# Both ends of a DLRM tower on one core: another treatment of a few contraction units in rounds -1, 0, 1, 29 and 30

## The chip, the core and the metric

The kernel runs on one NeuronCore of a Trainium2 chip. The metric is the device time of one execution in microseconds (us), the median of several runs. The engines are TensorE (PE; its weight loads are PEld), VectorE (DVE), ScalarE (ACT), GpSimd (POOL) and SyncE (SP), which issues most of the DMAs.

## What is computed

From 39 embedding tables rows of 16 numbers are gathered for a batch of 1024, giving `x` of 1024 x 39 x 16. Three layers of a compressed interaction network follow, and a small dense tower:

```python
def _cin(x, Ws, bs):
    h = x
    for i, (W, b) in enumerate(zip(Ws, bs)):
        Wr = W.reshape(F0, Fk, L)                              # L = 128
        z = jnp.einsum('bfd,bgd->bfgd', x, h)                  # products of every field with every row of h
        cur = jax.nn.relu(jnp.einsum('bfgd,fgl->bld', z, Wr) + b[None, :, None])
        if i != n - 1:
            h = cur[:, :L // 2]; direct = cur[:, L // 2:]
        else:
            direct = cur
        outs.append(direct)
    return jnp.concatenate(outs, axis=1).sum(-1)
...
h = jnp.concatenate([z, dense_ctx], axis=1)
h = jnp.maximum(h @ W_top1 + b_top1, 0.0)
h = jnp.maximum(h @ W_top2 + b_top2, 0.0)
y = h @ W_top3
```

## The kernel before, in words

The 1024 x 16 columns (batch, d) are cut into 32 steps of 512 columns. A step passes through layer 0, layer 1 and layer 2 in successive rounds: round `r` does layer 1 of step r+1 (units 0 to 9, `A_END`), layer 2 of step r (units 10 to 19, `C_END`) and layer 0 of step r+3 (units 20 to 23). Rounds run from -3 to 31; those at the ends lack some parts (`present`, line 57). Each unit is a pair of tiles of 128 products by 512 columns. VectorE makes the products `z` of a unit (line 628 for layers 1 and 2, line 679 for layer 0) and TensorE contracts them with the weights into one PSUM bank, over the ten units of a layer. ScalarE then applies bias and relu and writes `h1` or `h2`, the factor of the next layer's products, and the `direct` or `last` half, which VectorE sums over d (line 719).

How a unit is contracted depends on its kind (`KINDS`, `kind`, line 65):

- **F**, full: one fp32 matmul a tile, `wf` with `z` (line 1004). The trace records two instructions for each.
- **G, D, P**, split: ScalarE rounds `z` to `zh` (fp32r, line 826), a subtraction makes `zl = z - zh`, and TensorE adds three products a tile in fp32r: `wl` with `zh` (L1021), `wh` with `zh` (L1022), `wh` with `zl` (L1029). In G the subtraction is GpSimd's (L367), in D VectorE's (L715). In P the product goes to a PSUM bank half a unit at a time, and VectorE makes product (L694) and subtraction (L706) of each half, ScalarE rounding between (L811).

The order of the work is written out: each engine walks the rounds and units in the same order and waits on semaphores that count units. `z` has 7 buffers, `zh` and `zl` 4 each. VectorE does a D unit's subtraction `lag(r)` units after its product (1 before round 0, then 4, 2 in the last round). The second half of a P unit follows `half_lag` units later (line 109: 1 in round 30, otherwise 2). Before round 1 all split units are D, since P's bank is in use and GpSimd is busy: its queue holds 77 gathers of embedding rows ahead of its first subtraction, which is unit 11 of round 0. The last 38 of these wait for products of rounds -2 and -1 (`BESIDE`, line 148) and the two behind them. A few F units get split weights later (`wh_late`, `wl_late`): made by ScalarE and GpSimd in round 1 (unit 4, called `TENTH`) and in round 25 (units 3, 8, 14, 19).

In round 30 ScalarE writes the four later strips of `h2` (line 860) between its roundings; the `last` half of layer 2 (`take2`) stands at unit 1 of each round and waits for TensorE's last unit of the round before. After round 30 come the dense layers of the tower, then round 31 (layer 2 of the last step) and the last 128 rows.

## Time and profile before

| what | value |
|---|---|
| median of 3 runs | 1277.16 us (1276.98 to 1277.82) |
| profiled execution, own time | 1275.78 us |
| its span, first to last instruction | 1274.0 us |
| busy, share of the span | PE 95%, DVE 87%, POOL 84%, ACT 65% |
| mean granted TensorE clock | 0.997 |

All durations below come from the one profiled execution. Busy time counts instructions with work; a wait is idle time, and the profile names what ended it. TensorE's matmuls are pipelined, so a row of one matmul lasts longer than the distance to the next; the distance is what it costs in a row of them.

### The profile page before, as it was taken

What the parts mean: (1) busy time and instruction counts of PE and PEld (TensorE: products, weight loads), DVE (VectorE), ACT (ScalarE), POOL (GpSimd) and SP (SyncE); (2) the same over time, 40 slices, a digit from 0 to 9 for tenths busy, and PEclk for the clock granted to TensorE, in tenths of its full rate; (3) what the DMA queues carried; (4) which work ended last, traced back from release to release, by engine and by line L of the source; (5) the groups of instructions that cost most, each with busy time, mean ns of one, the idle gap of its engine ahead of it and who ended that gap; (6) DMA issues with size and microseconds to landing.
All of it is one profiled execution on the core that took longest, in us unless ns stands there. A gap on an engine that the chain in (4) does not pass through costs nothing.

```text
span 1274.0 us, 14489 instructions
## 1 busy us (share of the span) xinstructions
PE 1208.4 (95%) x4206; PEld 770.9 (61%) x4206; DVE 1113.7 (87%) x1274; ACT 829.4 (65%) x1129; POOL 1068.3 (84%) x643
## 2 busy tenths in 40 slices
PE   0588999999999999999999999999999999999899
PEld 0244566666666666666666666666666666766555
DVE  2189999899989999899999999899999999999763
ACT  1147666667676767666666767667766778777553
POOL 7467988898999999898999999898999878887533
PEclk9999999999999999999999999999999999999999
DMA  9194466654545556655545666554545666544100
GB/s 187 22 229 103 106 144 148 148 127 115 130 104 123 141 148 148 147 110 123 132 107 125 145 147 148 140 121 112 134 102 136 143 146 145 145 110 118 44 1 1
DMA packets 102511, 156.18 MB, mean 123 GB/s; under 512 B 20811, under 2 KB 32988, under 8 KB 102322
## 3 DMA queue, kind: packets, MB, share of 16 engines
q1 hardware_dynamic: 92256, 152.56, 50.0%
q0 software_dynamic: 10176, 2.70, 2.3%
q8 instruction: 33, 0.54, 0.2%
q14 instruction: 46, 0.38, 0.1%
HBM read 151.31 MB, written 6.19 MB: 124 GB/s over the span
## 4 chain that ended last, share of the span: by engine, by line
PE 82%; DVE 6%; POOL 4%; issue 4%; ACT 3%; DMA 0%; another core or an unknown queue 0%; DVEq 0%; ACTq 0%; POOLq 0%
PE curM L1004 35%; PE curM L1029 14%; PE curM L1021 14%; PE curM L1022 14%; POOL emb L356 3%; DVE z L628 3%; PE xk L993 2%; ACT h L860 1%; DVE zl L715 1%; ACT zh L826 1%; DVE zl L706 1%; POOL zl L367 1%; DVE z L679 0%; PE h L1127 0%; PE h L1135 0%
## 5 line engine op out<-in xcount | busy, mean ns | idle before, releaser
L367 POOL TENSOR_TENSOR zl<-z,zh 128x1024 fp32r<-128x1024 f32 (+1 forms) x314 | 749.7, 2398 | 106.6 <-ACT zh L826 94.1
L826 ACT ACTIVATE zh<-z 128x1024 fp32r<-128x1024 f32 (+1 forms) x333 | 351.5, 1057 | 312.4 <-DVE z L628 184.9
L628 DVE TENSOR_TENSOR z<-xr,h 128x1024 f32<-128x1024 f32 x456 | 548.7, 1212 | 3.8 <-issue 3.1
L1004 PE MATMUL curM<-z,wf 128*128 128x512 f32 (+3 forms) x1164 | 513.4, 600 | 0.9 <-ACT h L860 0.8
L356 POOL DMA_INDIRECT emb<-in_tbl_dram,idx x312 | 311.4, 998 | 88.1 <-issue 58.4
L1021 PE MATMUL curM<-zh,wl 128*128 128x512 f32 (+1 forms) x816 | 367.8, 451 | 4.0 <-issue 1.8
L1004 PEld LDWEIGHTS curM<-z,wf 128*128 128x128 f32 (+3 forms) x1164 | 204.2, 188 | 223.4 <-issue 206.5
L1022 PE MATMUL curM<-zh,wh 128*128 128x512 f32 (+1 forms) x816 | 320.5, 393 | 0.0
L1029 PE MATMUL curM<-zl,wh 128*128 128x512 f32 (+1 forms) x816 | 255.3, 394 | 10.3 <-POOL zl L367 6.0
L860 ACT ACTIVATE h<-curM,bias 64x512 f32<-64x512 f32 x372 | 240.4, 646 | 22.6 <-DVE z L628 11.2
L706 DVE TENSOR_TENSOR zl<-curY,zh 128x512 fp32r<-128x512 f32 x240 | 165.0, 688 | 63.5 <-ACT zh L811 58.5
L1021 PEld LDWEIGHTS curM<-zh,wl 128*128 128x128 f32 (+1 forms) x816 | 154.4, 189 | 59.8 <-issue 26.6
L1022 PEld LDWEIGHTS curM<-zh,wh 128*128 128x128 f32 (+1 forms) x816 | 153.8, 189 | 54.1 <-issue 26.1
L1029 PEld LDWEIGHTS curM<-zl,wh 128*128 128x128 f32 (+1 forms) x816 | 152.4, 188 | 51.2 <-POOL zl L367 8.7
L694 DVE TENSOR_TENSOR curY<-xr,h 128x512 f32<-128x512 f32 x240 | 166.1, 692 | 4.1
L811 ACT ACTIVATE zh<-curY 128x512 fp32r<-128x512 f32 x240 | 141.5, 590 | 15.8 <-PE curM L1029 6.5
L679 DVE TENSOR_TENSOR z<-xk,xs 117x1024 f32<-117x1024 f32 x116 | 120.7, 1081 | 1.2 <-PE curM L1004 1.2
L628 DVE TENSOR_TENSOR z<-xq,h 128x1024 f32<-128x1024 f32 x64 | 77.5, 1212 | 0.0
L860 ACT ACTIVATE direct<-curM,bias 64x512 f32<-64x512 f32 x62 | 42.4, 684 | 1.6
L993 PEld LDWEIGHTS xk<-ident,emb 128*117 128x117 f32 x120 | 28.5, 285 | 13.2 <-issue 8.5
L1021 PE MATMUL curM<-zh,wl_late 128*128 128x512 f32 x72 | 35.1, 487 | 0.0
L715 DVE TENSOR_TENSOR zl<-z,zh 128x1024 fp32r<-128x1024 f32 (+1 forms) x19 | 28.7, 1509 | 5.7 <-ACT zh L826 3.9
(140 smaller groups left out, 428.8 us busy)
## 6 DMA issues: line engine op xcount, KB each, us to landing
xr<-xT SPq DMA_DIRECT2D x384, 192.0 KB
xs<-xT SPq DMA_DIRECT2D x279, 156.0 KB
xq<-xT SPq DMA_DIRECT2D x64, 256.0 KB
emb<-in_tbl_dram,idx POOLq DMA_INDIRECT x312
xs<-xT SPq DMA_DIRECT2D x62, 78.0 KB
xT<-xc SPq DMA_DIRECT2D x31, 78.0 KB
xr<-in_L_rec_W_dram SPq DMA_DIRECT2D x16, 144.0 KB
xT<-xc SPq DMA_DIRECT2D x31, 40.0 KB
```

The lines of the kernel that those rows point to most:

```text
L356: nc.gpsimd.indirect_dma_start(out=emb[slot][:, f * D:(f + 1) * D], out_offset=None, in_=tables[f], in_offset=bass.IndirectOffsetOnAxis(ap ...
L367: nc.gpsimd.tensor_tensor(zl[0:n, SNUM[r, u] % NL, :], z[0:n, z_slot(r, u), :], zh[0:n, SNUM[r, u] % NH, :], ALU.subtract).then_inc(lo_poo ...
L628: return nc.vector.tensor_tensor(z[:, slot, :].rearrange("p (a n) -> p a n", a=2), x, h, ALU.mult)
L694: nc.vector.tensor_tensor(curY[:, :], xr[s % 2][:, q * N:(q + 1) * N], h[:, a * N:(a + 1) * N], ALU.mult).then_inc(done, 1)
L706: nc.vector.tensor_tensor(zl[:, SNUM[r, u] % NL, cols], curY[:, :], zh[:, SNUM[r, u] % NH, cols], ALU.subtract).then_inc(lo_dve if a == 1 ...
L811: nc.scalar.activation(zh[:, SNUM[r, u] % NH, a * N:(a + 1) * N], curY[:, :], ACT.Copy).then_inc(hi_ready if a == 0 else hi_second, 1)
L826: nc.scalar.activation(zh[0:n, SNUM[r, u] % NH, :], z[0:n, z_slot(r, u), :], ACT.Copy).then_inc(hi_ready, 1)
L860: nc.scalar.activation(dst, src, ACT.Relu, bias=bias).then_inc(done, 1)
L1004: mm = nc.tensor.matmul(cur[:, :], wf[rows, full_at(u), a, :], z[rows, z_slot(r, u), a * N:(a + 1) * N], start=start and i == 0, stop=stop ...
L1021: nc.tensor.matmul(cur[:, :], w_low[rows, w, a, :], zh[rows, h, cols], start=start and a == 0, stop=False)
L1022: nc.tensor.matmul(cur[:, :], w_high[rows, w, a, :], zh[rows, h, cols], start=False, stop=False)
L1029: mm = nc.tensor.matmul(cur[:, :], w_high[rows, w, a, :], zl[rows, l, a * N:(a + 1) * N], start=False, stop=stop and a == n - 1)
```

## The change

In the kinds, per round (before, then changed; kinds of units 0 to 9, 10 to 19, 20 to 23; all other rounds stay):

```
 -1 DDDFFDDDFF .......... FDFF      FEDFFDEDFF .......... FDFF
  0 DDDFFDDDFF FGDGFFGDGF FGFF      FEDFFDEDFF FGEGFFGEGF FGFF
  1 GPGFFGPGFF FGPGFFGPGF FGFF      FPGFFGPGFF FGPGFFGPGF FGFF
 29 GPGGFGPGFF FGPGGFGPGF ....      GPGFFGGGFF FGPGGFGGGF ....
 30 GPGGFGPGFF FGPGGFGPGF ....      FPGFFGGGFF FGPGGFGGGF ....
```

- A new kind **E** for units 1, 6, 12 and 17 before round 1: TensorE takes the high weights with all of `z` in fp32 and the low weights with `zh`; no `zl` is made. A buffer of `z` is then free only when TensorE is done with it.
- Unit 0 (`HEAD`) is F in rounds -1, 0, 1 and 30, and uses late split weights, made in round 1, in rounds 2 to 29.
- In rounds 29 and 30 unit 3 is F, and units 6 and 17 are G in place of P (`HANDED`).
- D units of round 0 have a lag of 2 in place of 4. The second half of a P unit always follows 2 units later.

```diff
-KINDS = "GPGFFGPGFF" + "FGPGFFGPGF" + "FGFF"
+KINDS = "FPGFFGPGFF" + "FGPGFFGPGF" + "FGFF"
...
-TENTH = 4
-LATE = (TENTH,) + LATE_C + LATE_A
-SHORT, LONGER = (STEPS - 3, STEPS - 2), (8, 19)
+HALF = 2
+TENTH, HEAD = 4, 0
+EARLY = (TENTH, HEAD)
+LATE = EARLY + LATE_C + LATE_A
+SHORT, LONGER, HANDED = (STEPS - 3, STEPS - 2), (3, 8, 19), (6, 17)
...
 def kind(r, u):
-    if r in SHORT and u in LONGER:
-        return "F"
-    if u == TENTH and 3 <= r < LATE_FROM and r % 4 != 2:
+    if r in SHORT and u in LONGER + HANDED:
+        return "F" if u in LONGER else "G"
+    if u == TENTH and 2 < r < LATE_FROM and r % 4 != 2:
+        return "G"
+    if u == HEAD and 2 <= r < STEPS - 2:
         return "G"
...
     if k == "P":
-        return "P" if r in IN_PSUM else "D"
+        return "P" if r in IN_PSUM else "E" if r < 1 else "D"
...
 def lag(r):
-    return 1 if r < 0 else 2 if r == LAST else 4
+    return 1 if r < 0 else 2 if r in (0, LAST) else 4
...
-def half_lag(r):
-    return 1 if r == STEPS - 2 else 2
...
 def behind(r, u, halves):
-    for n in (1, 2):
-        at = NUM[r, u] - n * halves
-        if at >= 0 and ORDER[at] in HALVES and half_lag(ORDER[at][0]) == n:
-            return ORDER[at]
-    return None
+    at = NUM[r, u] - HALF * halves
+    return ORDER[at] if at >= 0 and ORDER[at] in HALVES else None
...
(GpSimd; ScalarE the same with weight_hi_late)
-                    if (r, u) == (1, 2):
-                        weight_lo_late(0)
-                    if r == LATE_FROM and 2 <= u < 1 + len(LATE):
-                        weight_lo_late(u - 1)
+                    if r == 1 and 2 <= u < 2 + len(EARLY):
+                        weight_lo_late(u - 2)
+                    if r == LATE_FROM and 2 <= u < 2 + len(LATE) - len(EARLY):
+                        weight_lo_late(u - 2 + len(EARLY))
...
(VectorE, z_free)
-                if before is not None and kind(*before) == "F":
+                if before is not None and kind(*before) in "EF":
                     dve.wait_ge(z_used, NUM[before] + 1)
...
(TensorE, contract)
+                    if kind(r, u) == "E":
+                        pe.wait_ge(z_ready, NUM[r, u] + 1)
+                        for a in range(n):
+                            nc.tensor.matmul(cur[:, :], w_high[:, w, a, :].bitcast(F32), z[:, z_slot(r, u), a * N:(a + 1) * N],
+                                             start=start and a == 0, stop=False)
                     pe.wait_ge(hi_ready, SNUM[r, u] + 1)
+                    for a in range(n if kind(r, u) == "E" else 0):
+                        mm = nc.tensor.matmul(cur[:, :], w_low[:, w, a, :], zh[:, h, a * N:(a + 1) * N], start=False,
+                                              stop=stop and a == n - 1)
+                    if kind(r, u) == "E":
+                        mm.then_inc(z_used, 1)
+                        return
```

What VectorE issues for units 0 to 9 of round -1, before (`z` from `xr`, `xq` and `h` is a product, `zl` a subtraction):

```order
L628 TENSOR_TENSOR z<-xr,h 128x1024 x2
L715 TENSOR_TENSOR zl<-z,zh 128x1024
L628 TENSOR_TENSOR z<-xr,h 128x1024
L715 TENSOR_TENSOR zl<-z,zh 128x1024
L628 TENSOR_TENSOR z<-xr,h 128x1024
L715 TENSOR_TENSOR zl<-z,zh 128x1024
L628 TENSOR_TENSOR z<-xr,h 128x1024 x3
L715 TENSOR_TENSOR zl<-z,zh 128x1024
L628 TENSOR_TENSOR z<-xr,h 128x1024
L715 TENSOR_TENSOR zl<-z,zh 128x1024
L628 TENSOR_TENSOR z<-xr,h 128x1024
L715 TENSOR_TENSOR zl<-z,zh 128x1024
```

and the same place in the changed kernel, where the lines are numbered one lower:

```order
L627 TENSOR_TENSOR z<-xr,h 128x1024 x4
L714 TENSOR_TENSOR zl<-z,zh 128x1024
L627 TENSOR_TENSOR z<-xr,h 128x1024 x3
L714 TENSOR_TENSOR zl<-z,zh 128x1024
L627 TENSOR_TENSOR z<-xr,h 128x1024 x2
L714 TENSOR_TENSOR zl<-z,zh 128x1024
```

Six subtractions have become three, those of units 2, 5 and 7; the product of unit 9 (from `xq`) follows directly in both.

TensorE at the start of round 0, changed (the transposes of L992, then units 0, 1 and 2; before, all three units were the five rows that unit 2 still has):

```order
L992 MATMUL xk<-ident,emb 117x128 x4
L1003 MATMUL curM<-z,wf 128x512 x2
L1017 MATMUL curM<-z,wh 128x512 x2
L1021 MATMUL curM<-zh,wl 128x512 x2
L1031 MATMUL curM<-zh,wl 128x512
L1032 MATMUL curM<-zh,wh 128x512
L1031 MATMUL curM<-zh,wl 128x512
L1032 MATMUL curM<-zh,wh 128x512
L1039 MATMUL curM<-zl,wh 128x512 x2
```

Unit 0 needs `z` alone, and unit 1 (E) needs `zh` only for its last two matmuls.

ScalarE in round 30, units 0 to 3, before (`h` are the strips of `h2`, `last` waits for the end of round 29; `zh` from `curY` are halves of P unit 1):

```order
L860 ACTIVATE h<-curM,bias 64x512 x2
L811 ACTIVATE zh<-curY 128x512
L860 ACTIVATE last<-xk,bias 128x512
L860 ACTIVATE h<-curM,bias 32x512 x2
L811 ACTIVATE zh<-curY 128x512
L826 ACTIVATE zh<-z 128x1024
L860 ACTIVATE h<-curM,bias 32x512 x2
```

and changed:

```order
L859 ACTIVATE h<-curM,bias 64x512 x2
L810 ACTIVATE zh<-curY 128x512
L859 ACTIVATE last<-xk,bias 128x512
L859 ACTIVATE h<-curM,bias 32x512 x2
L825 ACTIVATE zh<-z 128x1024
L859 ACTIVATE h<-curM,bias 32x512 x2
L810 ACTIVATE zh<-curY 128x512
```

Unit 1's second half has moved behind `zh` of unit 2 and the last two strips of `h2`.

## Rows read from the trace of the kernel before

**Rows 1.** The page: busy us, share of the span and instructions of each engine.

```profile
PE 1208.4 (95%) x4206; PEld 770.9 (61%) x4206; DVE 1113.7 (87%) x1274; ACT 829.4 (65%) x1129; POOL 1068.3 (84%) x643
```

**Rows 2.** Stretches: length, busy of each engine (instructions), granted clock, DMA share, GB/s.

```profile
78.00:152.00 74.00, 63.15 (x194) 35.96 (x194) 70.94 (x64) 44.47 (x56) 62.17 (x44) 0.98 0.63 139
152.00:188.10 36.10, 36.10 (x125) 22.81 (x124) 34.51 (x40) 24.24 (x34) 31.86 (x21) 1.00 0.58 131
1186.40:1223.30 36.90, 31.84 (x110) 19.09 (x108) 26.77 (x32) 20.93 (x28) 21.33 (x9) 1.00 0.00 1
110.00:114.00 4.00, 3.71 (x10) 2.94 (x11) 4.00 (x5) 1.06 (x1) 3.39 (x3) 0.57 0.06 4
```

**Rows 3.** The chain of waits: start us, us, what; rounds -1 and 0.

```profile
95.91 3.40 DVE z L679 x3
...
137.16 3.43 PE curM L1004 x8
```

**Rows 4.** Timeline of VectorE: start us, us, instruction, count, idle before; rounds -1, 0.

```profile
77.47 2.35 DVE L628 TENSOR_TENSOR z<-xr,h 128x1024 f32<-128x1024 f32 x2 [3.06 <-issue]
...
111.28 1.22 DVE L715 TENSOR_TENSOR zl<-z,zh 128x1024 fp32r<-128x1024 f32 x1
...
123.75 5.75 DVE L628 TENSOR_TENSOR z<-xr,h 128x1024 f32<-128x1024 f32 x5
129.41 3.71 DVE L715 TENSOR_TENSOR zl<-z,zh 128x1024 fp32r<-128x1024 f32 x1
```

**Rows 5.** Timeline of TensorE, round 0 and the start of round 1.

```profile
108.11 0.47 PE L1021 MATMUL curM<-zh,wl 128*128 128x512 f32 x1 [1.78 <-issue]
...
132.08 0.74 PE L1029 MATMUL curM<-zl,wh 128*128 128x512 f32 x2 [1.86 <-POOL zl L367]
...
136.43 0.72 PE L1029 MATMUL curM<-zl,wh 128*128 128x512 f32 x2 [1.31 <-POOL zl L367]
...
141.81 0.39 PE L1021 MATMUL curM<-zh,wl 128*128 128x512 f32 x1
...
143.18 0.39 PE L1021 MATMUL curM<-zh,wl 128*128 128x512 f32 x1
...
151.94 0.87 PE L993 MATMUL xk<-ident,emb 128*117 128x128 f32 x4
```

**Rows 6.** GpSimd: its 38 gathers of 71 to 129.65 us grouped, then its timeline.

```profile
L356 POOL DMA_INDIRECT emb<-in_tbl_dram,idx x38 | 47.2, 1243 | 30.0 <-DVE z L679 19.4 <-issue 7.3 <-DVE z L628 3.4
...
100.90 0.94 POOL L356 DMA_INDIRECT emb<-in_tbl_dram,idx  x1 [0.30 <-issue]
...
111.36 1.96 POOL L356 DMA_INDIRECT emb<-in_tbl_dram,idx  x1 [0.30 <-DVE z L628]
...
129.66 2.37 POOL L367 TENSOR_TENSOR zl<-z,zh 128x1024 fp32r<-128x1024 f32 x1
132.18 1.77 POOL L356 DMA_INDIRECT emb<-in_tbl_dram,idx  x1 [0.16 <-issue]
```

**Rows 7.** Timeline of ScalarE, rounds -1 and 0: the activations into `h1` and `h2`.

```profile
95.94 4.00 ACT L860 ACTIVATE h<-curM,bias 64x512 f32<-64x512 f32 x6 [2.76 <-DVE z L628]
...
102.88 4.00 ACT L860 ACTIVATE h<-curM,bias 64x512 f32<-64x512 f32 x6 [1.25 <-DVE z L679]
```

**Rows 8.** Timeline of ScalarE, round 30.

```profile
1187.04 0.69 ACT L860 ACTIVATE last<-xk,bias 128x512 f32<-128x512 f32 x1 [2.15 <-PE xk L1004]
...
1189.01 0.57 ACT L811 ACTIVATE zh<-curY 128x512 fp32r<-128x512 f32 x1
```

**Rows 9.** Timeline of VectorE, round 30.

```profile
1191.97 0.69 DVE L719 TENSOR_REDUCE zq<-direct 128x128 f32<-128x512 f32 x1 [0.47 <-ACT h L860]
...
1205.93 0.69 DVE L706 TENSOR_TENSOR zl<-curY,zh 128x512 fp32r<-128x512 f32 x1 [1.07 <-ACT zh L811]
...
1217.80 1.21 DVE L628 TENSOR_TENSOR z<-xr,h 128x1024 f32<-128x1024 f32 x1
```

**Rows 10.** Timeline of TensorE, round 30: the start of unit 2.

```profile
1190.99 0.40 PE L1021 MATMUL curM<-zh,wl 128*128 128x512 f32 x1
```

More of the change, by code:

```diff
@@ L477, in round_ @@
                         for u in range(A_END + 3 * k + 1, A_END + 3 * k + 4):
-                            if kind(r, u) == "P" and u + half_lag(r) > A_END + 3 * k + 3:
+                            if kind(r, u) == "P" and u + HALF > A_END + 3 * k + 3:
                                 sp.wait_ge(z_second, HALVES[r, u] + 1)
@@ L910, in round_ @@
                             take0(r, i)
-                    if (r, u) == (1, 2):
-                        weight_hi_late(0)
-                    if r == LATE_FROM and 2 <= u < 1 + len(LATE):
-                        weight_hi_late(u - 1)
+                    if r == 1 and 2 <= u < 2 + len(EARLY):
+                        weight_hi_late(u - 2)
+                    if r == LATE_FROM and 2 <= u < 2 + len(LATE) - len(EARLY):
+                        weight_hi_late(u - 2 + len(EARLY))
                     if u == SPREAD_AT and r >= 1 and fresh(r) and r <= STEPS - 4:
@@ L1011, in contract @@
                         w, w_low, w_high = LATE.index(u), wl_late, wh_late
-                        if r <= LATE_FROM + 1 and (u != TENTH or r < 6):
+                        if r <= LATE_FROM + 1 and (u not in EARLY or r < 6):
                             pe.wait_ge(w_hi, HI_OPS + w + 1)
                             pe.wait_ge(w_lo, LO_OPS + w + 1)
-                    pe.wait_ge(hi_ready, SNUM[r, u] + 1)
+                    if kind(r, u) == "E":
[3 more added lines that the diff above has]
+                                             start=start and a == 0, stop=False)
+                    pe.wait_ge(hi_ready, SNUM[r, u] + 1)
+                    for a in range(n if kind(r, u) == "E" else 0):
[4 more added lines that the diff above has]
+                        return
                     for a in range(n):
```

## The prediction

> **What bounds the kernel now.** The page comes first [rows 1]: TensorE 95% busy, VectorE 87%, GpSimd 84%, so shares alone leave three candidates. The table by stretches separates them [rows 2]: in the 36.1 us of round 1, which stand for all the rounds up to 29, TensorE is busy for the whole stretch, so there only its own work counts. It idles in two places: rounds -1 and 0 (78 to 152 us: 63.2 of 74 us) and round 30 (1186.4 to 1223.3: 31.8 of 36.9 us). The change edits just these ends. All times below are on the clock of the trace of before.
>
> In round -1 the wait chain runs through VectorE, from 77.47 up to 95.91 [rows 3, 4]: products and subtractions (`zl`) follow one another without a gap. A product occupies it for 1.13 us (five from 123.75, next start 129.41), a subtraction for as long (1.22 with its overlap, like a product's 1.21) [rows 4]. In round 0 TensorE waits for GpSimd: for its subtraction of unit 11, begun at 129.66 behind the gathers, until 132.08, and for unit 13 until 136.43 [rows 5, 6]. From then on the chain is TensorE's own work [rows 3].
>
> **Prices on TensorE.** Two full units (F) take 3.43 us: 1.72 each [rows 3]. A three-pass unit (D, G, P) repeats after 141.81 at 143.18: 1.37, or 0.229 for each of its six matmuls of 512 columns [rows 5]. F in place of a three-pass unit costs 0.35. The new kind E has the fp32 matmuls of F and two short passes: 1.72 + 0.46 = 2.18, +0.81. No row shows an E; it lies between 1.72 (the short matmuls free) and 3.09 (they cost a whole three-pass unit), and since both parts have rows of their own shape I take 2.18. Weight loads lie beside the matmuls (PEld 61% busy) [rows 1]. Six E and six extra F are 4.9 + 2.1 = 7.0 us of new TensorE work.
>
> **Round -1.** Units 0, 1, 6 lose their subtractions, 3 x 1.13 = 3.4 us of VectorE's unbroken row. Unit 9's product releases the `h1` activations (95.94, 4.00 us); behind them stand `zh` of unit 21, its subtraction, the product of unit 23, and that releases the `h2` activations at 102.88, done at 106.88 [rows 7]. All are in one chain, so they move 3.4 earlier: 103.5. TensorE fits beneath: from 78.7, when unit 0's product (77.47, 1.2 us) is there, round -1 is 5 F + 2 E + 3 D = 17.1 us and 5.7 for units 20 to 23, ending near 101.5. Before, unit 0 of round 0 needed `zh` and started at 108.11 [rows 5]; as F it starts at 103.5.
>
> **Round 0 up to unit 11.** TensorE: 17.1 us for units 0 to 9, 1.72 for unit 10, 0.92 for unit 11's first passes: 123.2. GpSimd: 38 gathers stand ahead of its subtraction for unit 11 [rows 6]. One takes 0.94 and the pause 0.30, 1.25 together; all 38 took 47.2 us, 11.5 more than 38 x 0.94. The twelve long ones (up to 1.96) each start inside a VectorE subtraction and end 0.8 after it: 111.36 to 113.32 against the subtraction 111.28 to 112.50 [rows 4, 6]. Thirteen subtractions fall there now, seven remain (units 2, 5, 7 twice, and 21, which cost nothing before). Laying gathers of 1.25 us beside the new VectorE order gives extensions of 0.7, 0.8, 0.9, 0.4, 0.9, 0.9: 4.6 us. Bounds: 0 (all missed) and 6 x 1.02 = 6.1. So GpSimd is 11.5 - 4.6 = 6.9 us earlier (5.4 to 11.5), and unit 11's low part comes at 125.2. That is after TensorE's 123.2: GpSimd still decides, by 2.0 us.
>
> The Trainium skill (SBUF — State Buffer, section "SBUF: two separate sides") says a VectorE instruction with two SBUF inputs blocks only a GpSimd instruction that reads SBUF, and names two-port modes as what starves a DMA issued by GpSimd. By it these fp32 subtractions would not lengthen a gather, and the start would keep its 132.08; the rows above say otherwise, and I go by them.
>
> **Round 0 from unit 11.** Before, 132.08 to the end at 151.94 is 19.9 us, with 1.3 of waiting at unit 13. That wait came from the gather at 132.18 (1.77) inside unit 12's subtraction, itself held to 3.71 us by GpSimd [rows 4, 6]. Unit 12 is now E: no subtraction, and the wait goes. Two E add 1.6. 19.9 - 1.3 + 1.6 = 20.2: the round ends 6.9 - 0.3 = **6.6 us earlier**. VectorE sheds eight subtractions in the two rounds, but past unit 11 that wins nothing: it runs up against the seven `z` buffers and waits for TensorE. The lag of 2 instead of 4 for D units of round 0 costs nothing: `zh` of unit 2 is ready 2 units later. The loads for round 1 hang on ScalarE's `xc` copy of round 0, which moves along with unit 7, so they stay ahead of a round 1 that begins near 145.
>
> **Rounds 1 to 29.** TensorE-bound: unit 0 of round 1 costs +0.35, unit 3 of round 29 +0.35. One more pair of late weights (0.7 us on GpSimd, 0.4 on ScalarE) replaces a subtraction of 2.4 and one `zh`. Units 6 and 17 of round 29 go to GpSimd, 11 x 2.37 = 26.1 us in 29.4: hidden, with little spare.
>
> **Round 30.** TensorE ends round 29 at 1187.0, where it releases ScalarE's `last` [rows 8]; now at 1187.4. With the lag of one, unit 1's second half followed two activations (1189.01); with the lag of two it comes after `last`, two activations, `zh` of unit 2 and two more: 0.7 + 1.3 + 1.05 + 1.3 + 0.6, ready at 1192.4. VectorE's `zq` still waits for the last `h2` activation (1191.97) [rows 9], then comes unit 4's product, then unit 1's last half: 1194.3. So TensorE does unit 0 and half of unit 1, **idles 2.9 us and again 1.4**, and starts unit 2 at 1194.8 where it was 1190.99 [rows 10]: 3.8 later. Behind it, before, lay waits of 5.5 us (1190.99 to 1223.3 against 6 x 1.72 + 12 x 1.37 = 26.8), because VectorE stood 1.07 us at units 6, 12 and 17 and had half products besides [rows 9]. Now units 6 and 17 are whole and unit 12 has its lag: VectorE ends the round at about 1213 (1192.5 with 15 products, 5 halves and one sum behind) instead of 1219, ahead of TensorE. 7 x 1.72 + 11 x 1.37 = 27.1, plus 0.5 where GpSimd does units 5, 6, 7 in a row (3 x 2.37 from 1196.5, when units 4 and 5 have their products and `zh` is made, to 1203.6): 1222.4. Against 1223.3 a **gain of 0.9**, round 29's 0.35 included. Bounds: all 5.5 us stay, 1227.4 (4.1 lost); unit 1 does not wait, 1187.4 + 30.2 = 1217.6 (5.7 won). Round 31 and the top layers follow at TensorE's pace, unchanged.
>
> **Sum.** 6.6 - 0.35 + 0.9 = 7.1 us. The profiled execution took 1275.78 (span 1274.0): now 1268.7. The median of 1277.16, 1.4 above it, becomes 1270.1. A measurement of this kernel tells 0.2% from no change: 2.6 us, so faster means below 1274.6.
>
> **Rivals.**
> - First, the gathers miss the subtractions, and TensorE alone sets the start. Round 0 ends at 103.5 + 17.1 + 16.7 + 5.7 = 143.0, 8.9 earlier: 1267.7. For it: extension depends on phase. Chance 0.13.
> - Second, the wait at unit 1 of round 30 is much shorter than I lay out, up to 5.7 won there: 6.6 - 0.35 + 5.7 = 12.0, 1265.2. Against it: ScalarE works in program order. 0.07.
> - Third, the gathers are as long as before. Unit 11 gets its part at 132.1, and the sum is -0.3 - 0.35 + 0.9: 1276.9. This is also what the Trainium skill's rule above gives. Twelve rows in twelve speak against it. 0.07.
> - Fourth, the waits of round 30 stay behind the new one: 6.6 - 0.35 - 4.1 = 2.15 won, 1275.0. For it: GpSimd has ten subtractions there, as many as before. 0.08.
> - Fifth, slower: the clock. After waits in round 0 the granted clock was 0.57 in 110 to 114 us, mostly the 1.2 GHz level, where it is 1.00 in round 30 [rows 2]. The new waits in round 30 look alike. Priced as there it is (1 - 0.57) x 4 = 1.7 us, within my range. It turns the sign where over 9.7 us of full-speed work run at half; for half of the 27 us behind the wait, +13.5: 1283.6. 0.04. The Trainium skill (TensorE: Matmul & The Clock Gate, Part 1) has idleness bring back the half rate and activity lift it.
>
> The forecast keeps 0.61. Faster: 0.61 + 0.13 + 0.07, and what of the fourth lies beyond the limit, 0.83. Same: the third and most of the fourth, 0.13. Slower: 0.04. The range goes past the first rival on one side and to the fourth on the other, the start's lower bound (1.5 less) and the clock's 1.7 within it: 1266 to 1275.
>
> **What would show it.** TensorE's first F of round 0 near 103.5; the first GpSimd subtraction near 123 instead of 129.66; round 0's end near 145.5; long gathers six, not twelve. In round 30, an idle of some 3 us at unit 1 and hardly any after. Wrong if GpSimd's first subtraction does not move, if VectorE waits for loads before 103 us, or if round 30 keeps its later waits.

## The result, and the profile after

| | before | changed |
| --- | --- | --- |
| median of 4 runs, us | 1277.07 (1276.89 to 1277.82) | 1290.16 (1285.03 to 1296.93) |
| ratio | 1 | 1.011, 95% interval 1.008 to 1.0139 |
| profiled execution, us (span) | 1275.78 (1274.0) | 1286.04 (1284.0) |
| mean granted clock | 0.997 | 0.989 |

The change makes the kernel 13.1 us slower, and its runs scatter over 12 us where those of before lie within 1. Forecast were 1270.1 us and faster. Two executions of the changed kernel lie near 1285.5 (one is the profiled one) and two near 1295.6 (clock 0.984 and 0.985).

TensorE's transposes (L992, L993 before) open each round, so they date it (start in us). Before: round 0 at 105.46, round 1 at 151.94, round 28 at 1122.06, end at 1274.0. Changed: 102.62, 160.33, 1130.86, 1284.0. So round 0 opened 2.8 us earlier, **round 0 took 57.7 us in place of 46.5**, rounds 1 to 27 together 0.4 longer, and the rest 1.2 longer.

The page of the changed kernel, busy us and share of each engine, as [rows 1]:

```profile
PE 1216.3 (95%) x4194; PEld 772.3 (60%) x4194; DVE 1096.0 (85%) x1254; ACT 823.6 (64%) x1120; POOL 1060.5 (83%) x644
```

Stretches of the changed kernel: length, busy of each engine, granted clock, DMA share, GB/s, as [rows 2]:

```profile
78.00:103.00 25.00, 24.63 (x71) 12.80 (x69) 23.16 (x21) 14.37 (x19) 19.56 (x18) 1.00 1.00 227
103.00:161.00 58.00, 44.09 (x125) 24.14 (x125) 37.43 (x37) 27.91 (x37) 32.13 (x26) 0.85 0.39 84
116.70:133.80 17.10, 6.75 (x13) 3.31 (x12) 9.17 (x9) 5.32 (x8) 4.03 (x5) 0.50 0.16 34
161.00:197.00 36.00, 36.00 (x121) 21.99 (x121) 34.21 (x40) 24.42 (x34) 32.65 (x21) 1.00 0.54 131
1202.20:1209.00 6.80, 5.88 (x11) 3.81 (x12) 6.52 (x7) 3.17 (x3) 3.57 (x2) 0.50 0.00 0
```

In round -1 TensorE is busy for 24.6 of 25 us, as was wanted. In round 0 nobody is busy: TensorE 44 of 58 us, VectorE 37, GpSimd 32. In such a stretch the engines wait for one another, so the chain of waits has to be followed. The granted clock lies at 0.50, the 1.2 GHz level, for 17.1 us there and for 6.8 us in round 30.

Timeline of VectorE in round 0, as [rows 4]; idle time before in brackets:

```profile
105.05 1.20 DVE L627 TENSOR_TENSOR z<-xr,h 128x1024 f32<-128x1024 f32 x1
106.18 1.22 DVE L714 TENSOR_TENSOR zl<-z,zh 128x1024 fp32r<-128x1024 f32 x1
113.67 1.22 DVE L627 TENSOR_TENSOR z<-xr,h 128x1024 f32<-128x1024 f32 x1 [6.27 <-PE curM L1003]
116.50 1.22 DVE L627 TENSOR_TENSOR z<-xr,h 128x1024 f32<-128x1024 f32 x1 [1.61 <-issue]
125.64 1.22 DVE L627 TENSOR_TENSOR z<-xr,h 128x1024 f32<-128x1024 f32 x1 [7.93 <-remote]
126.78 1.22 DVE L714 TENSOR_TENSOR zl<-z,zh 128x1024 fp32r<-128x1024 f32 x1
```

Timeline of TensorE, the same stretch, as [rows 5]:

```profile
104.10 1.98 PE L1003 MATMUL curM<-z,wf 128*128 128x512 f32 x4 [0.61 <-issue]
...
109.49 3.59 PE L1003 MATMUL curM<-z,wf 128*128 128x512 f32 x8
116.03 0.50 PE L1031 MATMUL curM<-zh,wl 128*128 128x512 f32 x1 [2.95 <-issue]
...
128.06 1.22 PE L1039 MATMUL curM<-zl,wh 128*128 128x512 f32 x2 [10.28 <-DVE zl L714]
```

Timeline of GpSimd, as [rows 6]: the last of the 38 gathers, and GpSimd's first subtraction:

```profile
121.00 0.94 POOL L355 DMA_INDIRECT emb<-in_tbl_dram,idx  x1 [0.30 <-issue]
134.91 2.37 POOL L366 TENSOR_TENSOR zl<-z,zh 128x1024 fp32r<-128x1024 f32 x1 [12.96 <-ACT zh L825]
```

The three rows of products with a bracket are units 5, 6 and 7 of round 0. They wait for nothing but their buffer of `z` (unit 6 also for a load of `xr`, landed at 102.39): seven buffers back lie units 22 and 23 of round -1 and unit 0 of round 0, all F, whose buffer is free when TensorE has counted them in the semaphore `z_used`. (A count, below, is such an update of a semaphore.) Unit 0 ran from 104.10 on. Yet unit 7's product, which needs its count, starts at 125.64. TensorE stands still meanwhile, 10.28 us, for the subtraction of unit 5, which is in VectorE's queue behind the product of unit 7. So what is missing is the count. The trace records when TensorE's semaphores are raised; beside them, the end of the last matmul of each unit (not printed by the views, read from the same trace, us):

```
                               last matmul ends   count arrives   late
before   round 0, unit 0            111.51            114.87       3.4
         round 0, unit 1            113.91            114.94       1.0
         round 0, unit 3            117.27            117.28       0.0
changed  transposes of round 0      103.49            123.50      20.0
         round 0, unit 0            106.08            125.62      19.5
         round 0, unit 1            108.26            125.70      17.4
         round 0, unit 4            113.08            125.89      12.8
         round 0, unit 5            129.28            129.29       0.0
```

TensorE's counts arrive up to **20 us late**, in order, and then five in 0.27 us. Some 100 of the 768 counts of `z_used` have no record. A record belongs to the latest unit that the records behind it leave for it, or to an earlier one, so each lateness of `z_used` here is the least that it can be. In steady state, and from 129 us on, they come 0.01 to 0.02 us after the matmul. Before the change there was a lateness too, of 3.4 us, and it cost little. The Trainium skill (Perfetto Trace Analysis, section "Tensor Engine Instruction (MATMUL, LD_WEIGHTS)") has the count pushed when the last bytes in PSUM are acknowledged, and the end of a matmul in a profile only estimated. The steady rounds agree; no rule of it gives the 20 us.

### The profile page after: what moved, and what is told of

Read it like the earlier page. It is cut to its first block, busy times and chain, and to the rows that moved or that the text cites. A ratio compares the mean times of both kernels' runs of the same rounds, so it can differ in the third digit from the quotient of the medians.

```text
span 1284.0 us, 14414 instructions
## 1 busy us (share of the span) xinstructions
PE 1216.3 (95%) x4194; PEld 772.3 (60%) x4194; DVE 1096.0 (85%) x1254; ACT 823.6 (64%) x1120; POOL 1060.5 (83%) x644
## 4 chain that ended last, share of the span: by engine, by line
PE 89%; DVE 3%; issue 3%; POOL 2%; ACT 2%; another core or an unknown queue 1%; DMA 0%; DVEq 0%; ACTq 0%
PE curM L1003 38%; PE curM L1039 14%; PE curM L1031 14%; PE curM L1032 14%; POOL emb L355 2%; PE xk L992 2%; DVE z L627 2%; ACT h L859 1%; PE curM L1017 1%; PE h L1089 1%; PE curY L1003 1%; ACT zh L825 1%; DVE zl L705 1%; PE h L1137 0%
## 5 line engine op out<-in xcount | busy, mean ns | idle before, releaser
L1003 PE MATMUL curM<-z,wf 128*128 128x512 f32 (+3 forms) x1188 | 525.7, 601 | 1.9 <-issue 1.0
L1031 PE MATMUL curM<-zh,wl 128*128 128x512 f32 (+1 forms) x740 | 335.3, 453 | 5.7 <-issue 2.9
L1032 PE MATMUL curM<-zh,wh 128*128 128x512 f32 (+1 forms) x740 | 290.8, 393 | 0.1
L1039 PE MATMUL curM<-zl,wh 128*128 128x512 f32 (+1 forms) x740 | 230.8, 393 | 11.6 <-DVE zl L714 10.3
L705 DVE TENSOR_TENSOR zl<-curY,zh 128x512 fp32r<-128x512 f32 x232 | 159.5, 687 | 57.7 <-ACT zh L810 52.6
L1031 PEld LDWEIGHTS curM<-zh,wl 128*128 128x128 f32 (+1 forms) x740 | 139.7, 189 | 59.1 <-issue 28.4
L1032 PEld LDWEIGHTS curM<-zh,wh 128*128 128x128 f32 (+1 forms) x740 | 139.7, 189 | 52.0 <-issue 25.8
L1039 PEld LDWEIGHTS curM<-zl,wh 128*128 128x128 f32 (+1 forms) x740 | 139.5, 189 | 44.7 <-DVE zl L714 11.2
L1031 PE MATMUL curM<-zh,wl_late 128*128 128x512 f32 x124 | 58.3, 470 | 0.0
L1032 PE MATMUL curM<-zh,wh_late 128*128 128x512 f32 x124 | 48.6, 392 | 0.0
L1039 PE MATMUL curM<-zl,wh_late 128*128 128x512 f32 x124 | 38.5, 392 | 0.0
```

What stands on the lines that cost most here:

```text
L705: nc.vector.tensor_tensor(zl[:, SNUM[r, u] % NL, cols], curY[:, :], zh[:, SNUM[r, u] % NH, cols], ALU.subtract).then_inc(lo_dve if a == 1 ...
L1003: mm = nc.tensor.matmul(cur[:, :], wf[rows, full_at(u), a, :], z[rows, z_slot(r, u), a * N:(a + 1) * N], start=start and i == 0, stop=stop ...
L1031: nc.tensor.matmul(cur[:, :], w_low[rows, w, a, :], zh[rows, h, cols], start=start and a == 0, stop=False)
L1032: nc.tensor.matmul(cur[:, :], w_high[rows, w, a, :], zh[rows, h, cols], start=False, stop=False)
L1039: mm = nc.tensor.matmul(cur[:, :], w_high[rows, w, a, :], zl[rows, l, a * N:(a + 1) * N], start=False, stop=stop and a == n - 1)
```

## The experiments

Theory A at this point: E and F units free their buffer by TensorE's late count, D units by VectorE's own, so E turns a harmless lateness into a standstill. The rival, B, is the end (round 30, at half clock for 6.8 us). In the diffs `-` is the change as made, or the kernel that the text names as the one started from. The table of all runs is at the end of this section.

**Halves of the change.** Only the start:

```diff
-SHORT, LONGER, HANDED = (STEPS - 3, STEPS - 2), (3, 8, 19), (6, 17)
+SHORT, LONGER, HANDED = (STEPS - 3, STEPS - 2), (8, 19), ()
-    if u == HEAD and 2 <= r < STEPS - 2:
+    if u == HEAD and 2 <= r:
```

with `half_lag` of before.

> The change's start (E in rounds -1 and 0, unit 0 as F there, lag 2 in round 0) with the end of before (SHORT, LONGER, HANDED, half_lag, unit 0 as G in rounds 29 and 30). Theory A: the loss is VectorE's standstill in round 0, where it waits for TensorE's count of used buffers (6.3, 1.6 and 7.9 us in the trace of the change), and the half clock that follows: this kernel then lies at 1277 plus 8.8 (what the change's trace is behind at round 28), near 1286 and as scattered as the change (1285 to 1297). Rival B: the end carries the loss, since round 30 of the change has 6.8 us at the lower clock level: this kernel then lies near 1270.

Measured 1287.12 us (1284.72 to 1297.53). The start alone carries the loss; rival B falls. The profiled execution is the slowest of the five, and in it the standstill is not in round 0, as theory A had it, but already in round -1: VectorE waits for counts from 92 us on, 8.92 and 7.17 us the longest, and round 0 opens only at 121.34. Where the standstill falls differs from one execution to another; the scatter of the changed kernel may be the same thing, but none of its slower executions was traced.

**No E**, lag 4 in round 0:

```diff
-        return "P" if r in IN_PSUM else "E" if r < 1 else "D"
+        return "P" if r in IN_PSUM else "D"
-    return 1 if r < 0 else 2 if r in (0, LAST) else 4
+    return 1 if r < 0 else 2 if r == LAST else 4
```

> The change without E: units 1, 6, 12, 17 of rounds -1 and 0 are D again and round 0 has lag 4; unit 0 stays F in rounds -1 to 1 and the end stays as changed. Theory A (E's buffers are freed by TensorE's count instead of VectorE's own, and that is what makes VectorE stand): back to within 2 us of before, 1274 to 1278. Rival B (the end or unit 0 as F loses): 1279 or more. Rival C (any F more in round 0 makes VectorE wait by TensorE's count): a standstill of VectorE in round 0 stays, of over 3 us.

Measured 1284.57 (1283.64 to 1285.07). Theory A falls as stated: without a single E, VectorE stands at the product of unit 10, as rival C foresaw, for an F unit's count:

```profile
129.08 1.22 DVE L627 TENSOR_TENSOR z<-xq,h 128x1024 f32<-128x1024 f32 x1 [8.96 <-remote]
```

**E in round -1 alone** (`"E" if r < 0`, lag 4 in round 0).

> E in round -1 alone; round 0 has D and lag 4 as before. Theory A: round -1 keeps its gain (the first product of round 0 2.8 us earlier than in before) and VectorE's buffers of round 0 come free by its own subtractions: 1272 to 1275, faster than before. Rival B (E itself is dear wherever it stands, or delays TensorE's count already in round -1): 1277 or more, with a wait of VectorE of over 3 us in round 0.

Measured 1289.45 (1286.98 to 1296.51). Now it is ScalarE that waits for a late count, between rounds, for unit 9 of round -1:

```profile
113.10 0.68 ACT L859 ACTIVATE direct<-curM,bias 64x512 f32<-64x512 f32 x1 [13.78 <-remote]
```

**No E, lag 2.**

> As the kernel without E, but round 0 with lag 2 as in the change. Theory A: within 2 us of the kernel without E. Rival (the shorter lag makes VectorE wait for ScalarE's high parts): 2 us or more slower than that one, with waits of VectorE for zh in round 0.

Measured 1277.15 (1274.97 to 1278.7), 7.4 us faster than with lag 4. Both expectations fail. A lag moves no work; it only moves VectorE's subtractions to other moments. What such a move changes for somebody else is GpSimd's gathers, which a subtraction lengthens [rows 6]. In all these traces the counts are latest where gathers go out at one in 1.25 us, without a long one between. Of the gathers between 104 and 118 us one starts every 1.40 us with lag 4 and every 1.47 with lag 2, and 118 to 132 us every 1.25 and 1.66.

So theory G: **gathers issued back to back hold TensorE's counts up.** Before the change, VectorE's subtractions broke the row: twelve gathers were long. The change took away six of the thirteen subtractions beside the gathers, and four long ones are left.

**Four kernels for theory G.** The control, which leaves GpSimd to its gathers alone through round 0:

```diff
-    return "D" if k == "G" and (r < 0 or (r == 0 and u < POOL_FROM)) else k
+    return "D" if k == "G" and r < 1 else k
```

> The change with one edit: no subtraction of round 0 on GpSimd (G of round 0 is D), so that GpSimd does nothing but its 38 gathers until round 1. It is the control of the three kernels sent with it. TensorE's count of used buffers and of transposes stays late in rounds -1 and 0 as in the change (there up to 18 us): a standstill of VectorE or ScalarE of over 5 us in round 0 by every theory; 1280 to 1297.

Measured 1288.66 (1287.09 to 1291.04). The transposes of round 0, ended at 103.78, are counted at 127.79, 24.0 us late; the four counts just before are of units of round -1, the first of them late by 28.6 us at the least. VectorE stands three times:

```profile
111.43 1.22 DVE L627 TENSOR_TENSOR z<-xr,h 128x1024 f32<-128x1024 f32 x1 [10.01 <-remote]
117.77 1.22 DVE L627 TENSOR_TENSOR z<-xr,h 128x1024 f32<-128x1024 f32 x1 [5.11 <-remote]
127.58 1.22 DVE L627 TENSOR_TENSOR z<-xr,h 128x1024 f32<-128x1024 f32 x1 [8.59 <-PE curM L1003]
```

Paced, the control with a fill behind each gather, into a part of `zs` that is written much later:

```diff
+            def pace(f):
+                pool.wait_ge(paced, f)
+                nc.gpsimd.memset(zs[:, 1, B - PACED:B], 0.0).then_inc(paced, 1)
...
                 gather(f, 1, gathered[1])
+                pace(f)
```

> The control with GpSimd filling 512 columns between each two gathers, so that a gather is issued every 1.6 to 2 us instead of every 1.25. Theory G (gathers issued back to back, no longer slowed by VectorE's subtractions, are what holds TensorE's counts back): the counts come late by under 4 us and VectorE's standstills in round 0 go, so round 0 ends 8 us or more earlier than in the control and the time is under 1277 plus what late gathers cost round 1. Rival E (it is E's own instructions, or the dense stream of TensorE, whatever GpSimd does): the counts stay late by over 8 us, the time stays within 4 us of the control.

Measured **1268.73** (1267.47 to 1269.19), ratio 0.994 (0.9923 to 0.9956): 20 us below the control and 8 below before, by an instruction that does nothing for the result. Rival E falls: E and the dense TensorE are as in the control. GpSimd's timeline in round -1, a gather every 1.66 us:

```profile
95.16 0.95 POOL L357 DMA_INDIRECT emb<-in_tbl_dram,idx  x1 [0.17 <-issue]
96.11 0.54 POOL L364 MEMSET zs<- 128x512 f32 x1
96.81 0.95 POOL L357 DMA_INDIRECT emb<-in_tbl_dram,idx  x1 [0.17 <-issue]
```

and round 0, with TensorE busy for 39.7 of 40.3 us at full clock:

```profile
103.00:143.30 40.30, 39.68 (x122) 22.06 (x121) 40.27 (x39) 27.78 (x36) 36.83 (x46) 1.00 0.54 120
```

All counts recorded from 78 us on come at most 0.02 us after the matmul.

Late, the control with all 38 gathers behind the first product of unit 10 (`pool.wait_ge(z_ready, NUM[0, A_END] + 1)` ahead of them).

> The control with all 38 gathers moved behind the first product of unit 10 of round 0. Theory G: no gather runs between about 70 and 115 us, TensorE's counts come within 0.1 us of the matmul in all of that stretch, round -1 and the first half of round 0 run without a standstill, and the lateness appears only behind the gathers' new start, if at all. Rival E: lateness and standstill as in the control, at 85 to 128 us.

Measured 1298.66 (1295.22 to 1299.08), since TensorE now waits 27.7 us for the gathered rows at round 1. What it tells is the stretch before the first gather:

```profile
118.08 0.94 POOL L355 DMA_INDIRECT emb<-in_tbl_dram,idx  x1 [65.84 <-DVE z L628]
```

Up to there counts are at most 0.02 us late, and neither VectorE nor TensorE stands for longer than `h` and `zh` take. As theory G has it. Behind it the lateness reaches only 0.33 us (at 125.26) up to 144, which the last two kernels take up.

Plain, with `pool.dma_start` of the first 128 rows of each table in place of the indexed gather.

> The control with the 38 gathers of the second block replaced by plain copies of the first 128 rows of each table, issued on the same engine (so the rows of block 1 are other rows). Theory G with the gathers' own issue as the cause: lateness goes or falls under 2 us, since a plain copy takes GpSimd less and writes fewer descriptors by index. Rival (any DMA that GpSimd starts): lateness stays over 5 us.

This kernel leaves the ids of the second block out, so its result is of other rows. Measured 1268.18 (1267.06 to 1269.43), counts 0.02 us late at most. As many bytes by the same engine's queue do no harm, at a higher rate even: all 39 copies are issued between 71 and 103 us. A copy takes GpSimd 0.53 to 0.58 us where a gather takes 0.94, so this run does not tell the index from GpSimd's longer work on each. That GpSimd is merely busy is not it: the paced kernel keeps it busier than the control (0.95 + 0.54 of 1.66 us against 0.94 of 1.25).

**How fast is too fast, what the start and round 30 are worth.** Three kernels from the paced one: fills of 128 and of 256 columns, and round 30 mended; and the same two edits (paced, no subtraction on GpSimd in round 0) in the kernel before.

> The kernel before with the two edits of the paced one (GpSimd fills 512 columns between gathers; no subtraction of round 0 on GpSimd). Theory G: in before TensorE's count was late by 3.4 us once (114.87 us), which cost ScalarE a wait of 2.5 us; pacing takes it away, and what is left of the difference to the paced change (1268.7) is what E, unit 0 and the new end are worth when the counts come in time: 1272 to 1277, 4 to 8 us above the paced change. Rival: pacing and D in round 0 are the whole gain, and this kernel comes to within 1.5 us of 1268.7.

Measured 1279.96 (1274.92 to 1280.81). With the counts prompt, the old start and end are 11.2 us slower than the changed ones (paced_D): TensorE waits eleven times in rounds -1 and 0 for a subtraction, 6.0 us in all. It also says that pacing, with the subtractions of round 0 on VectorE, wins nothing without the change: this kernel is 2.8 us slower than before. Neither end of my expectation came.

> The paced change with 128 columns between gathers instead of 512: a gather every 1.3 to 1.4 us. If the rate decides, the counts come late again (over 3 us) and the time lies between 1270 and 1289; if any instruction between two gathers is enough, counts prompt and 1268 to 1269.

Measured 1271.26 (1267.73 to 1275.25): counts up to 9.0 us late (the unit that ended at 120.53 is counted at 129.52), and the scatter is back. A gather every 1.33 us is still too fast.

> The paced change with 256 columns between gathers: a gather every 1.4 to 1.5 us. If the rate decides: lateness under that of 128 columns, or none; the time at or below that of 128 columns. If prompt, the gathers end earlier than with 512 and the time is 1267.5 to 1269.

Measured 1268.19 (1265.08 to 1268.45), counts prompt, with one every 1.44 us at least:

```profile
108.42 0.95 POOL L357 DMA_INDIRECT emb<-in_tbl_dram,idx  x1 [0.17 <-DVE z L636]
109.38 0.33 POOL L364 MEMSET zs<- 128x256 f32 x1
109.87 0.95 POOL L357 DMA_INDIRECT emb<-in_tbl_dram,idx  x1 [0.17 <-issue]
```

Round 30:

```diff
+    if (r, u) == (STEPS - 2, 1):
+        return "D"
-    return 1 if r < 0 else 2 if r in (0, LAST) else 4
+    return 1 if r < 0 else 2 if r in (0, STEPS - 2, LAST) else 4
-                    if u == 3 and r >= 0:
+                    if r >= 0 and u == (8 if r == STEPS - 2 else 3):
                         sum_direct(r)
```

> The paced change with unit 1 of round 30 as D at lag 2 instead of P, and VectorE's sum of direct in round 30 behind unit 8 instead of unit 3. In the paced trace TensorE waits 2.77 us (ScalarE's second half behind four activations of h) and 1.27 us (VectorE's second subtraction behind the sum) there, and 3.4 us at half clock follow, about 1.5 us. Theory: both waits and the half clock go, 4 to 5.5 us: 1263 to 1265. Rival: the product of a later unit or ScalarE's high parts are late next, and under 2 us are gained.

Measured 1264.66 (1264.09 to 1265.0), 4.1 us below the paced one. What TensorE waited for from round 28 to the end, in the paced kernel (us in total, times, longest):

```profile
PE curM L1042 <- ACT zh L821: 2.8, 1, 2.8
PE curM L1050 <- DVE zl L714: 1.3, 1, 1.3
PE curM L1014 <- ACT h L870: 0.3, 1, 0.3
```

and in this one:

```profile
PE curM L1052 <- POOL zl L374: 1.3, 1, 1.3
PE curM L1016 <- ACT h L872: 0.3, 1, 0.3
```

Both waits went, the 3.4 us at half clock with them, and a wait of 1.3 for GpSimd came.

**The change as it is, but paced**; its parts once more, with prompt counts; and the sum of what was found. In the first, only the 36 gathers that stand beside rounds -2 and -1 get a fill of 256 columns, and GpSimd keeps its subtractions of round 0.

> The change whole and as it is, GpSimd's subtractions of round 0 included, with one edit: GpSimd fills 256 columns behind each gather that stands beside rounds -2 and -1. Theory: the change itself is sound and only the late counts turn it over: 1268 to 1274, faster than before; against the paced one without GpSimd's subtractions in round 0 (1268.2) it pays what TensorE waits for GpSimd at unit 11, up to 6 us, since the gathers end later. Rival: TensorE's wait there pulls the clock down and the kernel is no faster than before.

Measured 1278.06 (1274.91 to 1279.59), ratio 1.001 (1.0001 to 1.0019): the rival. This is 12.1 us below the change, by nothing but the fills, so the late counts are nearly all that the change loses to before. Counts are prompt, but the gathers end at 126.6 and GpSimd's first subtraction is late, so TensorE stands at unit 11, and the clock is at 0.5 from 125.1 to 131.9. The profiled execution is the fastest of eleven:

```profile
129.06 1.22 PE L1048 MATMUL curM<-zl,wh 128*128 128x512 f32 x2 [7.60 <-POOL zl L372]
```

> The paced change (512 columns) with the end of before. The prediction gave the new end a gain of 0.2 us (0.9 less 0.35 twice); with prompt counts its round 30 has the same two waits of TensorE as before plus 3.4 us at half clock. If the clock takes the end's gain, this kernel is within 0.5 us of 1268.7; if the prediction's gain at the end holds, up to 1 us slower; if the new end loses by itself, 1 us or more faster.

Measured 1268.53 (1267.95 to 1269.71): level with the new end (1268.73), so the 11.2 us above are the start's.

> The paced change (512 columns) with D in place of E, lag 2 kept. With prompt counts E's worth stands alone: by the prediction's rows, three subtractions less in round -1 (4.6 us of start) and VectorE ahead in round 0: 4 to 9 us slower than 1268.7, 1272 to 1278. Rival: unit 0 as F and the pacing carry the gain, and this one is within 2 us of 1268.7.

Measured 1274.35 (1273.59 to 1275.55): E is worth 5.6 us once the counts are prompt.

The last has the fills of 256 columns and the mended round 30.

> The paced change with 256 columns, unit 1 of round 30 as D and the sum of direct behind unit 8 there. The two gains lie in different rounds and should add: 1263.5 to 1264.5. Rival: with 256 columns some run meets late counts, and the median rises over 1265.

Measured **1263.28** (1261.04 to 1264.27), ratio 0.9893 (0.9878 to 0.9908): 13.9 us below before, the fastest of all.

**Does a row build up?** Two kernels from the control, neither paced. In one the row of gathers starts later; in the other it is broken once:

```diff
+            pool.wait_ge(z_ready, NUM[-1, 5] + 1)
             for f, ru in enumerate(BESIDE):
```

```diff
-                pool.wait_ge(z_ready, NUM[ru] + 1)
+                pool.wait_ge(z_ready, NUM[(0, 0) if f >= 16 else ru] + 1)
```

> The control without pacing, but with the block's gathers started behind the product of unit 5 of round -1, near 86 us instead of 71. In the late_D run gathers ran back to back (1.25 us) from 118 to 145 us beside a full TensorE and its counts were at most 0.33 us late, in the control they were 28 us late at 127. If lateness builds up with every gather of an unbroken row, wherever it stands: late by 1 us from about 100 us on and over 5 us by 125, a standstill in round 0, over 1278. If only rows that begin beside round -2 or so do it: prompt, near 1268 plus what the later gathers cost round 1.

(The expectation has late_D's row unbroken from 118 us on; it had three long gathers, of 1.7 to 1.8 us, up to 134.) Measured 1297.67 (1294.75 to 1302.4). Gathers from 86.8 on; the last prompt count recorded is of 100.33, then the transposes that ended at 103.61 are 5.2 us late and the unit that ended at 109.77 by 32.2 at the least. In the end TensorE itself falters in the middle of units, with the products of both units there since 128.07:

```profile
131.41 1.01 PE L1004 MATMUL curM<-z,wf 128*128 128x512 f32 x1 [0.93 <-issue]
133.51 1.01 PE L1004 MATMUL curM<-z,wf 128*128 128x512 f32 x1 [1.09 <-issue]
136.31 1.01 PE L1004 MATMUL curM<-z,wf 128*128 128x512 f32 x1 [1.79 <-issue]
```

> The control without pacing, with one pause: the first 16 gathers as they are, the other 20 behind the first product of round 0, near 100 us. If the lateness is a backlog that a pause empties: late by about 1 us before 92 us, prompt from the pause on, and under 3 us late by 128; 1267 to 1272. If it does not empty, or builds up within 20 gathers: over 5 us late and over 1275.

Measured 1267.7 (1266.15 to 1269.16), 21 us below its control by one wait moved. The row broken:

```profile
91.25 0.94 POOL L355 DMA_INDIRECT emb<-in_tbl_dram,idx  x1 [0.30 <-issue]
99.60 0.94 POOL L355 DMA_INDIRECT emb<-in_tbl_dram,idx  x1 [7.41 <-DVE z L627]
```

At 90.52 a count is 7.6 us late at the least. The unit that ended at 87.71 is counted at 93.01, 5.3 late; within 0.22 us three more follow, the last for a matmul that ended at 92.99. From the pause on all are within 0.02 us, through the other 20 gathers, whose row is broken anew by long ones (1.6 to 1.9 us) beside VectorE's subtractions. A backlog, then, that a pause of GpSimd empties. That fits late_D too: long gathers broke its row at first, and its unbroken part started near 138 us, 6 us before TensorE ran out of work.

| kernel | median us | round 0, us | latest count, us, at the least |
| --- | --- | --- | --- |
| before | 1277.1 | 46.5 | 3.4 |
| changed | 1290.2 | 57.7 | 20.0 |
| start_only | 1287.1 | 52.0 (opened at 121.34) | 28.7 |
| no_E / no_E_lag2 | 1284.6 / 1277.2 | 53.3 / 46.8 | 14.2 / 4.6 |
| E_round_m1 | 1289.5 | 61.7 | 25.7 |
| ctrl_D / mid_D | 1288.7 / 1297.7 | 64.0 / 67.4 | 28.6 / 32.2 |
| late_D | 1298.7 | 68.4 | 0.3 |
| paced_128 | 1271.3 | 46.4 | 9.0 |
| paced_256 / paced_D | 1268.2 / 1268.7 | 40.6 / 40.7 | 0.0 |
| plain_D / pause_D | 1268.2 / 1267.7 | 40.6 / 40.7 | 0.0 / 7.6, then 0.0 |
| before_paced_D | 1280.0 | 48.0 | 0.0 |
| paced_no_E | 1274.4 | 44.7 | 0.0 |
| paced_old_end / paced_D30 | 1268.5 / 1264.7 | 40.6 / 40.6 | 0.0 |
| change_paced | 1278.1 | 49.9 | 0.0 |
| best | 1263.3 | 40.6 | 0.0 |

Round 0 is from its transposes to those of round 1 in the profiled execution; the lateness is that of rounds -1 and 0.

## Why the prediction was wrong, point by point

- **Prices.** F 1.72, three passes 1.37, E 2.18. Held: an E of round -1 starts at 80.97, the next unit at 83.15, 2.18.
- **Round -1.** Forecast: the first F of round 0 at 103.5, was 104.10, and TensorE full beneath. Held.
- **GpSimd.** Forecast: 6.9 us earlier. Its last gather starts at 121.00 and it would have been free at 121.9, near the forecast 123. Its first subtraction, the sign that the prediction named, came at 134.91 instead, since it waited for `zh` of a unit whose product was late. Six long gathers were foreseen; four longer than 1.4 us came, each beside a subtraction of VectorE as before (106.79 to 108.22 beside 106.18 to 107.40). The size held, and the meaning was wrong: the long gathers were priced as 11.5 us of pure loss. They were also the only breaks in the row, and paced_D makes every gather 0.4 us dearer and gains 20 us.
- **Round 0, the step that failed.** "VectorE sheds eight subtractions ..., but past unit 11 that wins nothing: it runs up against the seven `z` buffers and waits for TensorE." The step let a buffer be free as soon as TensorE is done with it, and the sum of 17.1 us for TensorE's units 0 to 9 held no wait for VectorE at all. VectorE ran against the buffers already at unit 5, for 6.3 + 1.6 + 7.9 us, because the counts came up to 20 us late behind GpSimd's row of gathers; TensorE lost 2.95 + 10.28 us in return and then ran at the lower clock level. Forecast was an end of round 0 that comes 6.6 us earlier; it came 8.4 us later. With prompt counts and no subtraction on GpSimd (paced_D) it is 40.7 us long, 5.8 less than before, and opens at 102.65, 2.8 earlier.
- Was it to be seen? In the trace of before ScalarE waits 2.50 us at 114.95 for TensorE's count, which nothing in TensorE's timeline explains: the unit had ended 3.4 us earlier. My working read the engines' rows and never set a wait against the end of what it waited for. The row gave the size beside the old, often broken row of gathers; that it would grow sixfold no row told.
- **Round 0 from unit 11, GpSimd deciding.** The change never got that far. change_paced did, and there a wait of 7.6 us stood in place of the forecast 2.0, with gathers of 1.44 us in place of 1.25. No run has prompt counts, gathers at 1.25 us and GpSimd's subtractions in round 0 together, so whether the 2.0 us would have come stays open.
- **The lag of 2 in round 0**, put at nothing. Without E it was worth 7.4 us (no_E and no_E_lag2), by where it put the subtractions beside the gathers.
- **Rounds 1 to 29.** Forecast +0.35 and +0.35, measured +0.41 (rounds 1 to 27) and +0.36 (28 and 29). Held.
- **Round 30.** Forecast: idle 2.9 and 1.4 at unit 1. Measured 2.77 and 1.27. The round was to take 35.0 us; from the end of round 29's last matmul to the end of its own it took 37.15 (before 36.42), 6.8 us of it at half clock; in the paced kernel 35.83, with 3.5 us at 0.51. The fifth rival had priced the clock at 1.7 us there. With prompt counts the new end is level with the old (paced_D and paced_old_end), not better: what the shorter waits give, the clock takes back, 1.7 us by half of 3.4 (an estimate). [rows 2] had a clock of 1.00 in round 30, where before's waits were short and scattered.
- **Rivals.** The sign was the fifth's, 1283.6, with half the loss, but by luck: in round 0 half clock followed the standstill (from 116.7 us, VectorE's first wait ended at 113.67) and did not cause it. My chance of 0.04 for slower had one mechanism behind it and none for a late semaphore.

What stays open: which path in the chip gathers and TensorE's counts share. The runs show that gathers by index in an unbroken row of 1.25 or 1.33 us do it, that 1.44 us, a break or plain copies don't, and that VectorE's, ScalarE's and GpSimd's own counts show nothing of it (0.02 us at most in the changed kernel, ctrl_D and mid_D). Whether it needs a TensorE as dense as here wasn't tried. A hint that it doesn't: in all these kernels, before included, the gathers of the first 128 rows of the batch go out unpaced, and TensorE's first transposes, some 3 us behind them, are counted 1.4 to 3.4 us late (before: ended at 55.21, counted at 57.50), with TensorE busy for 10 of the 18 us from 40 to 58.

## What to carry to other kernels

An instruction that waits long for an engine that has long been done is a finding in itself: set each wait's end beside the end of the work it waits for, before counting what a change wins. When GpSimd issues a long row of gathers, keep the row broken, with useful work if there is any, and look again after every change that takes work from the engine that used to slow it. And put work that relies on a tight ring of buffers where its releases are prompt. Freeing most of the buffers by the engine's own count did not help here: without E VectorE still stood for 8.96 us, at one F unit.

## What the runs showed of the hardware that was not expected

- TensorE's semaphore updates came up to 28.6 us (ctrl_D) and 32.2 us (mid_D) after the matmul, at the least, in order, and drained at one in 0.04 to 0.08 us once GpSimd's row of gathers broke or ended: 3.7 us after the end of the last gather in the changed kernel, 4.5 in ctrl_D, 0.8 behind the sixteen gathers of pause_D.
- The limit in this kernel lies between 1.33 us (9.0 us late) and 1.44 us (0.0 late) from gather to gather of 128 rows of 64 bytes; the bare gather takes 1.25. A fill of 0.33 us on GpSimd costs 0.19 us of that rate, since the gap of 0.30 before the next gather shrinks to 0.17.
- While counts are held up long enough, gaps come between TensorE's own matmuls too, inside a unit whose products and weights are there (0.9 to 1.8 us, mid_D).
- After waits of 2.77 and 1.27 us in round 30 the clock was at 0.5 for 3.4 us in some traces and for 6.8 in others.
- The Trainium skill (SBUF — State Buffer, section "SBUF: two separate sides") holds that engine ports and DMA ports are disjoint and that neither can slow the other there. The lateness is in no conflict with it if it lies in the path of semaphores or descriptors and not in SBUF; no run here tells which.
